# A two-layer graph network on one core: edges over 128 partitions of 420 (padded) instead of 125 of 425

## What is computed

```python
x = x + _L0_gnn_ref(_layernorm(x, axis=-1), edge_index, edge_attr_64, L0_gnn_Wq, ...)
x = x + _L0_ffn_ref(_layernorm(x, axis=-1)[None], L0_ffn_W1, ...)[0]
x = x + _L1_gnn_ref(_layernorm(x, axis=-1), L1_gnn_W1, L1_gnn_W2, L1_gnn_b, src, dst)
x = x + _L1_ffn_ref(_layernorm(x, axis=-1)[None], L1_ffn_Wr, ...)[0]
```

## Time and profile before

| | |
|---|---|
| three runs | 2831.36, 2835.22, 2837.24 us; median 2835.22 |
| span of the profiled execution | 2837.5 us |
| POOL busy | 1360.6 us (48%) |
| PE, DVE, ACT busy | 1546.7, 1139.1, 753.7 us |
| DMA | 438.71 MB, 155 GB/s over the span |

### The profile page before, as it was taken

The page is one execution under the profiler, slowest core; times in us unless marked ns, Lnnn a source line. Parts: engine busy times, 40 slices in busy tenths (PEclk is TensorE's granted clock), DMA queues, the critical chain, the costliest instruction groups (busy, mean ns, idle before and its releaser), DMA issues. The chain is left out here.

```text
span 2837.5 us, 37033 instructions
## 1 busy us (share of the span) xinstructions
PE 1546.7 (55%) x8939; PEld 1343.6 (47%) x8940; DVE 1139.1 (40%) x2742; ACT 753.7 (27%) x1817; POOL 1360.6 (48%) x1158
## 2 busy tenths in 40 slices
PE   5608777778771398599930000000002765999992
PEld 3307666767660355399920000000001655999992
DVE  6416666665664632211142333333333674212113
ACT  2305545444450133243420000000000122433330
POOL 4248888888870300022206888788886001222220
PEclk9857877776775599799965555555555957999996
DMA  6277444444444100155545666666654015999997
GB/s 160 66 151 142 127 124 125 125 123 126 124 104 95 46 26 18 33 184 196 196 123 154 169 168 165 165 168 169 168 165 124 7 46 190 342 341 345 333 345 207
DMA packets 339784, 438.71 MB, mean 155 GB/s; under 512 B 107805, under 2 KB 280098, under 8 KB 339623
## 3 DMA queue, kind: packets, MB, share of 16 engines
q1 hardware_dynamic: 204257, 288.71, 33.2%
q0 software_dynamic: 129248, 146.40, 19.4%
q10 hardware_dynamic: 6242, 3.19, 0.8%
HBM read 346.24 MB, written 90.90 MB: 154 GB/s over the span
## 5 line engine op out<-in xcount | busy, mean ns | idle before, releaser
L1637 POOL DMA_INDIRECT fr<-f_rows,src_s x425 | 523.7, 1232 | 185.2 <-issue 129.6
L654 POOL DMA_INDIRECT qr<-q_rows,src_s x425 | 527.7, 1242 | 158.8 <-issue 129.0
L1920 PE MATMUL psO<-acc,carry_on 125*125 125x256 f32 x50 | 21.7, 616 | 741.1 <-DVEq L1816 723.2
L1657 DVE SCALAR_TENSOR_TENSOR acc<-acc,same,fr 125x256 f32<-125x256 f32 x425 | 206.6, 486 | 455.6 <-DMA fr<-f_rows,src_s 395.5
L1920 PEld LDWEIGHTS psO<-acc,carry_on 125*125 125x125 f32 x50 | 14.9, 310 | 747.6 <-DVEq L1816 723.6
L749 PE MATMUL psK<-kp,oh_k 126*125 x1700 | 331.8, 375 | 6.3 <-issue 3.6
L749 PEld LDWEIGHTS psK<-kp,oh_k 126*125 126x125 bf16 x1700 | 308.2, 195 | 26.2 <-issue 20.0
L818 DVE TENSOR_TENSOR qr<-qr,psK 125x512 f32<-125x512 f32 (+1 forms) x255 | 142.8, 595 | 224.4 <-DMA qr<-q_rows,src_s 108.2
L1458 PEld LDWEIGHTS m1psH<-m1xT,m1w 128*128 128x128 f32 x1792 | 211.1, 194 | 2.8
L1458 PE MATMUL m1psH<-m1xT,m1w 128*128 128x128 f32 x1792 | 211.4, 277 | 0.0
L1470 PE MATMUL m1psY<-m1w,m1hT 128*128 128x256 f32 x896 | 203.1, 380 | 1.4 <-issue 0.9
(11 more groups left out here) (419 smaller groups left out, 2452.0 us busy)
## 6 DMA issues: line engine op xcount, KB each, us to landing
m1w<-in_L_ffn_W_dram SPq DMA_DIRECT2D x112, 1024.0 KB
run_rows<-acc SPq DMA_DIRECT2D x85, 560.0 KB
m0w<-in_L_ffn_Wd_dram SPq DMA_DIRECT2D x32, 1024.0 KB, 5.2
loc<-locals_ SPq DMA_DIRECT2D x86, 153.8 KB
ea<-in_edge_attr_dram SPq DMA_DIRECT2D x85, 140.0 KB
yt<-y SPq DMA_DIRECT2D x15, 560.0 KB
m1b<-in_L_ffn_b_dram SPq DMA_DIRECT2D x56, 128.0 KB
qr<-q_rows,src_s POOLq DMA_INDIRECT x425
```

The costliest lines, as they stand in the source:

```text
L654: nc.gpsimd.indirect_dma_start(out=qr[:, g, u, :], out_offset=None, in_=q_rows, in_offset=bass.IndirectOffsetOnAxis(ap=src_s[:, g, u:u + 1 ...
L1637: nc.gpsimd.indirect_dma_start(out=fr[:, g, u, :], out_offset=None, in_=f_rows, in_offset=bass.IndirectOffsetOnAxis(ap=src_s[:, g, u:u + 1 ...
L1657: ins = nc.vector.scalar_tensor_tensor(acc[:, g, u, :], acc[:, n // G % G, n % G, :], same[:, bass.ds(i * G * G + g * G + u, 1)], fr[:, g, ...
```

## The change

The edges are padded: 128 partitions (E) of J = 420, that is 53760 places for 53125 edges. Partitions 0 to 125 (FULL = 126) are full, partition 126 holds REST = 205 edges, and 127 holds none. NK falls to 84 groups, loops are unrolled by GI = 4 (4 slots instead of 5 in `qr`, `loc`, `ea`, `fr`, `acc`) and turned 21 times; indices are staged 2 groups ahead instead of 3, and `oh_k` has 2 slots instead of 3. The tiles of the score stage hold ET = 127 edges and a dummy row with index 0, so that a gather takes 128 rows while one-hots over CB = 4 blocks of 42 still cover a tile. All gathers (L329, L654, L1026, L1637, L1731) write 128 rows; the scatter L337 stays at 125. The core of the diff:

```diff
-J = N_EDGES // P
-EITER = J // (G * G)
+E = 128
+J = 420
+PADS = E * J - N_EDGES
+FULL = N_EDGES // J
+REST = N_EDGES - FULL * J
+ET = 127
+GI = 4
 NK = J // G
-AHEAD = 3
+EITER = NK // GI
+AHEAD = 2
...
-                sp.dma_start(dst_i[:], dst_p).then_inc(s_dst, 16)
+                sp.wait_ge(s_pad, 1)
+                sp.dma_start(dst_i[0:FULL, :], dst_p).then_inc(s_dst, 16)
+                sp.dma_start(dst_i[FULL:FULL + 1, 0:REST], rest(dst)).then_inc(s_dst, 16)
...
-                sp.dma_start(src_g[:], src.rearrange("(k e) -> k e", k=NK)).then_inc(s_src, 16)
+                sp.wait_ge(s_pad, 3)
+                sp.dma_start(src_g[0:NK - 1, :], src[0:(NK - 1) * G * ET].rearrange("(k e) -> k e", k=NK - 1)).then_inc(s_src, 16)
+                sp.dma_start(src_g[NK - 1:NK, 0:N_EDGES - (NK - 1) * G * ET],
+                             src[(NK - 1) * G * ET:N_EDGES].rearrange("(k e) -> k e", k=1)).then_inc(s_src, 16)
...
+                nc.vector.memset(dst_i[96:E, :], N_NODES).then_inc(s_pad, 1)
+                nc.vector.memset(src_g[64:NK, :], 0).then_inc(s_pad, 1)
+                nc.vector.memset(src_i[96:E, :], 0).then_inc(s_pad, 1)
+                v.wait_ge(s_dst, 48)
...
+                nc.vector.memset(part_i[96:E, :], 0)
+                nc.vector.memset(end_i[96:E, :], 0)
+                nc.vector.memset(local_g[:], 0.0)
+                link(nc.vector.memset(src_t[:], 0))
...
-            src_s = sb(st, "src_s", [P, G, G], I32)
-            qr = sb(st, "qr", [P, G, G, D])
+            src_s = sb(st, "src_s", [E, GI, G], I32)
+            qr = sb(st, "qr", [E, GI, G, D])
...
-            K_SLOT = (0, 1, 0, 1, 2)
+            K_SLOT = (0, 1, 0, 1)
...
+                    sp.wait_ge(s_ead, i * GI + g + 1)
+                    sp.dma_start(ea[0:112, g, :], eav[0:112, at]).then_inc(s_ea[g], 16)
+                    sp.dma_start(ea[112:FULL, g, :], eav[112:FULL, at]).then_inc(s_ea[g], 16)
+                    if tail:
+                        sp.dma_start(ea[FULL:FULL + 1, g, :], ear[:, at]).then_inc(s_ea[g], 16)
+                    else:
+                        sp.sem_inc(s_ea[g], 16)
...
+                nc.vector.memset(ea[:], 0.0).then_inc(s_eaz, 1)
...
+                dve_order.link(v, nc.vector.tensor_scalar(counts[0:1, 0, 0:1], counts[0:1, 0, 0:1], -float(PADS), None, ALU.add))
...
-                for a, b in HALVES:
-                    sp.dma_start(dot[a:b], dot_rows.rearrange("h (p j) -> p h j", p=P)[a:b]).then_inc(s_dot, 16)
+                sp.wait_ge(s_dotz, 1)
+                for a, b in ((0, 112), (112, ET)):
+                    sp.dma_start(dot[a:b], dot_rows.rearrange("h (p j) -> p h j", p=ET)[a:b]).then_inc(s_dot, 16)
...
+                nc.vector.memset(dot[96:E], 0.0).then_inc(s_dotz, 1)
...
-                        for a, b in HALVES:
-                            sp.dma_start(to[a:b, bass.ds(i * G * G + g * G, G), :], acc[a:b, g]).then_inc(s_accst, 16)
-                        sp.wait_ge(s_accst, (i * G + g + 1) * 32)
+                        sp.dma_start(to[:, bass.ds(i * GI * G + g * G, G), :], acc[:, g]).then_inc(s_accst, 16)
+                        sp.wait_ge(s_accst, (i * GI + g + 1) * 16)
```

More of the change, by code:

```diff
@@ L219, in build @@
             par = sb(st, "par", [X * KC, 4, 128])
[L220 to L225, removed]
+            prev_i = sb(st, "prev_i", [E, 1], I32)
+            prev_f = sb(st, "prev_f", [E, 1])
+            begins = sb(st, "begins", [E, J])
+            rank_e = sb(st, "rank_e", [E, J])
+            run_pre = sb(st, "run_pre", [E, 1])
+            rank_g = sb(st, "rank_g", [NK, G * ET])
             base_f = sb(st, "base_f", [NK, G])
@@ L561, in _ @@
                     third_part(i)
-        score = sb(top, "score", [P, H, J])
-        s_webd, s_ea = sem("we_loaded"), [sem(f"ea{g}_loaded") for g in range(G)]
+        score = sb(top, "score", [E, H, J])
+        s_eaz = sem("ea_zeroed")
+        s_webd, s_ea = sem("we_loaded"), [sem(f"ea{g}_loaded") for g in range(GI)]
         s_staged, s_open = sem("indices_staged"), sem("gathers_open")
-        s_got = [sem(f"rows{g}_gathered") for g in range(G)]
-        s_loc = [sem(f"locals{g}_loaded") for g in range(G)]
+        s_got = [sem(f"rows{g}_gathered") for g in range(GI)]
+        s_loc = [sem(f"locals{g}_loaded") for g in range(GI)]
         s_kp = [sem(f"k_parts{n}_loaded") for n in range(3)]
@@ new lines, in load_locals @@
+                def load_locals(i, g):
+                    sp.wait_ge(s_kt, i * GI + g + 2)
+                    sp.wait_ge(s_kta, i * GI + g + 2)
+                    sp.dma_start(loc[:, (g + 1) % GI, :], locals_[bass.ds((i * GI + g + 1) * G * E, G * E)]
+                                 .partition_broadcast(3 * R)).then_inc(s_loc[(g + 1) % GI], 16)
+                last_i, last_g = REST // G // GI, REST // G % GI
+                with sp.Fori(0, last_i) as i:
+                    for g in range(GI):
+                        load_ea(i, g, True)
+                        load_locals(i, g)
@@ L639, in _ @@
+                for g in range(GI):
+                    load_ea(last_i, g, g < last_g)
+                    load_locals(last_i, g)
+                with sp.Fori(last_i + 1, EITER) as i:
+                    for g in range(GI):
+                        load_ea(i, g, False)
+                        load_locals(i, g)
                 for part in range(2):
@@ L649, in _ @@
                 with pool.Fori(0, EITER) as i:
[L650 to L651 removed]
+                    for g in range(GI):
+                        pool.wait_ge(s_staged, i * GI + g + 1)
                         pool.sem_inc(s_open, 1)
@@ L1632, in _ @@
                 with pool.Fori(0, EITER) as i:
-                    for g in range(G):
-                        pool.wait_ge(s_st7, i * G + g + 1)
+                    for g in range(GI):
+                        pool.wait_ge(s_st7, i * GI + g + 1)
                         pool.sem_inc(carrier, 1)
```

378 lines of the change are left out of this document (187 added, 191 removed).

## The result

The changed kernel takes **2582.2 us** (median of 4 runs, 2574.8 to 2588.6) against 2834.7 for the kernel before: ratio 0.911, 95% interval 0.909 to 0.913. The profiled execution took 2574.8 us.

What follows compares the result with a forecast made beforehand. POOL's gathers were taken to bound the sum and score stages, with the compute chain late next in the latter. Terms summed to -191.3 us, 2837.5 to 2646.2; with the profiled execution 2.3 above the median, 2644 us, range 2590 to 2696.

Steps and rivals of the forecast that it cites:

- What bounds each stage: POOL's gathers alone set the sum stage's end and the score stage's pace; the compute chain would be late next in the latter.
- Price of a gather: All gathers of the change on POOL: 1.276 us each, taken from L1404's pace; bounds 1.27 and 1.52 us.
- Sum stage: Layer-1 gathers, L1637: 420 starts at POOL's new pace span 534.6 us instead of 652.0, -117.4 us.
- Score stage: Q gathers, L654: the compute chain's own 7.01 us a group becomes the limit, 587.6 us instead of 643.4, -55.8 us.
- Rival A: In the score stage the compute chain follows POOL to 6.38 us a group: another 52 us less, 2592 us, chance 0.17.
- Turning back: Stores and loads after the score stage: idling taken as the price of 89-row chunks goes, -18 us, bounds 0 and -22.
- Denominators, `dot`, join: Cheaper gathers save 2.4 us in the denominators and 3 us in the join; clearing 32 partitions of `dot` adds 3.3 us.
- Start: Preparation ahead of the score stage: clears of small tiles and transfers of other shapes add 2 us, bounds -4 and +12.
- Rival D: The 83-row load of `src_g` gets stuck on one DMA engine, delaying `rank_g`: 10 us more, 2654 us, chance 0.13.
- B: Gathers in the two big loops, L654 and L1637, do not get cheaper: 2807 us, chance 0.06.
- C: A store or the DMA engines bound the sum stage at 7.0 us a group: 52 us more, 2696 us, chance 0.10.
- E: Gathers no cheaper, and POOL runs dry with 4 slots and 2 groups ahead: slower, 2891 us, chance 0.02.

## Why the prediction was right and wrong

- **What bounds each stage: right.** The sum stage belongs to POOL before and after. In the score stage POOL set the pace before, and the compute chain was late next.
- **Price of a gather: right, by luck of the reference row.** 1.276 us from L1404 against 531.2/419 = 1.268. The reason was missing: that row happened to have the new divisor as well as the new row count. The prediction used the divisor for the stores of 89 and 84 rows and the load of 83, and never asked what it says of 125.
- **Sum stage: right**, -120.8 for -117.4.
- **Score stage: the step that failed.** "In that stretch the compute chain ran at its own pace: ... 7.01 us each" took ten intervals of one execution for the chain's pace. The mechanism (chain late next, DVE waiting for PE) held; the term was mis-sized. The chain's own pace is 6.3 us once it runs, and a second profile of the same ten groups gives 6.61, of which 0.5 are waits for gathers, so "never for a gather" was not safe either. Of the 58.4 us missed, 82 intervals x (7.01 - 6.334) are 55.4; the other 3 lie in the first interval (9.8 us instead of 12.8). A pace under 6.5 us was the prediction's own sign of being wrong, and it came.
- **Rival A** came nearest (2592 us, 10 above the measured time) by a mechanism half right. The chain does not follow POOL wherever it goes; it has a limit of its own, PE's queue, that lies where POOL now lies. With 0.17 it was given too little: its price had one row behind it, the 7.01 only ten intervals.
- **Turning back: right in cause and size**, -15.6 for -18.
- **Denominators, `dot`, join: within the noise.** DVE's wait for `dot` grew from 2.9 to 5.9 us as forecast, yet the stretch around it did not get longer. The stretch up to the first `fr` gather varies between 535.0 and 540.5 us in two profiles of the kernel after, so its -4.1 means little.
- **Start: wrong in sign, small.** 1.8 us lie before the first scatter, most of the rest while K is loaded. Padding the gathers alone brought 209.3 to 207.1, leaving four of five out 200.6, so gathers issued during the load of K delay it. A second profile of the kernel before has 210.7. Rival D did not come: DVE waited 7.5 us for `rank_g`, not more than the 8.2 before.
- Rivals B, C and E are out by the gathers' mean, the sum stage's pitch and the sign.

What stays open is why an indirect DMA's time on POOL follows the divisor, and why the 64-row gather took 1.34 us as a group's last and 0.92 as its first.

## What to carry to other kernels

Look at the largest divisor up to 16 of every partition count that a DMA moves, gathers and scatters included: one dummy row (125 to 126) was worth most of this change, while a gather of 127 rows costs 2.56 us against the 1.21 of 125. A pace read from ten noisy intervals is a guess; take another stretch or profile, or price the rival by it. When one engine gets faster, the next limit may lie a tenth of a microsecond behind, so measure the chain with the old limit taken out.

## What the runs showed that was not expected

- POOL's time for an indirect gather of 1 KB rows goes from 0.95 us (128 rows) to 2.56 us (127 rows), near 0.87 + 1.69/n us for a largest divisor n (113 rows lie 0.19 us below that); a scatter of 125 rows has a mean of 1283 ns, of 128 rows 1063.
- PE's granted clock between 300 and 720 us was higher where groups came faster: 0.71 and 0.73 in two profiles of the kernel before (7.6 us a group), 0.79 in the one with padded gathers alone (6.37). K's matmuls had means of 389 and 375 ns in the first two and 357 in the third. Whether this cost any time, no run here shows: POOL set the pace in the slower ones.
- A bf16 weight load of 126x127 had a mean of 185 ns, of 126x128 122 ns, with no clear effect on the time here.
- A DVE cast of 0.37 us took 15.27 us beside a POOL clear of 16.09 us.
- Adding 63 ns to the mean of 1680 weight loads, and taking 321 of 406 us of Q gathers from POOL, each left the time where it was; moving some 2 us of register loads a group cost about 30 us.
- POOL's DMA queue moved 129248 packets where gathers had 125 rows and 56368 where they had 128, for nearly the same bytes.
